# VectorE, not TensorE, sums the gathered relation messages in a graph network kernel

## The chip, the cores and the metric

The kernel runs on one core of one Trainium2 chip. The metric is the time on the device in microseconds, from one launch that computes everything. The engines are named as the profile names them: PE is TensorE, DVE is VectorE, ACT is ScalarE, POOL is GpSimd, SP is SyncE.

## What is computed

The reference runs three layers of a graph network over 3125 nodes with 128 features and 103125 edges, then adds the input and normalises. In each layer every node sums two things over its incoming edges:

```
ht = einsum('nd,rdo->nro', h, W_rel[l]);  msg = ht[src, etype]
h_rel = segment_sum(msg, dst) + h @ W_loop[l] + b_rel[l]
z = (h @ W_gat[l]).reshape(n, H, DH)
e = leaky_relu(el[src] + er[dst], 0.2);  ex = exp(e - segment_max(e, dst)[dst])
h_gat = segment_sum(ex / segment_sum(ex, dst)[dst] * z[src], dst) + b_gat[l]
hc = concatenate([h_rel, h_gat]) @ W_fuse + b_fuse
h = relu(hc * gate if l == 0 else hc)
```

The plain sum of `msg` is the "relation sum"; the sum weighted by the attention `ex` is the "attention sum". The change concerns the relation sum.

## The kernel before

**Tables and gathers.** For each layer a table in HBM has one row per node and relation: 128 numbers of the message, 128 of z and 4 attention terms `el` (`ROW` = 260 numbers). Nodes are ranked by degree and put in 25 tiles of 128, one node to a partition. A tile needs as many slots as its largest node has edges; a slot is one row per partition. POOL fetches one slot of a tile with one indirect DMA (`gather`, L640).

**Groups.** Slots are worked in groups of 8 in the buffers `A` and `B`, and at a tile's end a tail: `t8` (8 slots, in `scratch`) and `t7` (up to 7 slots, gathered in pieces of 4, 2 and 1, `pieces`). A tile is therefore A, B, perhaps one or more further pairs A, B, then perhaps t8 and t7. In all there are 348 groups. An empty slot of `t7` has its attention term set to `LEAST`, so that its weight is zero.

**One group.** The DVE (`group`, L1454 on) waits until the slots have landed, makes the logits in six short steps (`raw`, `top`, `leaky`, `peak`, the kept top, `logit`, L1471 to L1483), and waits for ACT to turn them into weights `wgt` (L863) and weight columns of `zx` (L864). Then it multiplies z by the weights into `zx` (L1487), rescales the running sum `acc` (L1489), does the `meanwhile` work of that group, and when PE has summed the group (`s_gat`) adds PE's sum to `acc` (L1495). PE (`group`, L1103 on) waits for the landed slots and adds their messages into `ps_rel`, one matmul with the identity per slot (`relation_sum`, L1112); then it waits for `zx` and sums it over the slots in the same way into `ps_gat` (L1126). A float32 matmul is two records in the trace, so a group of 8 has 16 of each kind. The first matmul of L1126 releases the buffer to POOL (`s_free`), the last one signals `s_gat`.

**Tile and table work.** At a tile's end DVE inverts the denominators and forms `hr` (relation sum plus loop term, L1509) and `hg` (L1513). The rest of that tile, its epilogue, is done inside the next tile: PE transposes `hr` and `hg` (L1135, L1136) behind the relation sum of A, ACT evacuates them, PE multiplies by W_fuse; in layer 0 a gate follows (L1151) behind the relation sum of B; in layers 0 and 1 PE then computes the next table's rows (`ps_z` L948, `ps_tab` L958) around the third and fourth group. ACT evacuates these in program order with the weights of the groups, so that a group's weights can stand behind them. `stage_tails`, called in A's `meanwhile`, copies the indices of the tail, fills `t7` (L1436) and signals `s_tail`; POOL waits for that before it gathers a tail.

**Order.** Nothing reorders this: each engine's instructions stand in the order in which its block writes them, with semaphores between. POOL's gathers go on as long as the next buffer is free.

## Time and profile before

| | |
|---|---|
| median of 3 runs | 4862.06 us (4856.94 to 4863.91) |
| the profiled execution | 4824.77 us, of which the span of instructions is 4823.2 us |
| busy, share of the span | PE 49%, PE weight loads 41%, DVE 25%, ACT 11%, POOL 53% |
| DMA | 517.47 MB, mean 107 GB/s |

The page gives each engine's busy time and its share of the span, the span in 40 slices, the chain of work that ended last, and the costliest groups of instructions. In the chain, "issue" is time in which the engine waited for nothing that the profile shows, and "another core or an unknown queue" (also "remote") is a wait whose releasing signal came at a time at which the profile knows no instruction that ended; this program has one core. The end of a matmul in the records is modelled; the time at which its signal arrives is not.

### The profile page before, as it was taken

Reading aid. Unit: us, or ns where it says so; the run is one execution under the profiler, and the core shown is the slowest. Engines: PE = TensorE matmul, PEld = TensorE weight load, DVE = VectorE, ACT = ScalarE, POOL = GpSimd, SP = SyncE. Lnnn points to the kernel's source line nnn. Section 1 sums busy time; section 2 is a strip of 40 time slices with the busy share of each in tenths; the row PEclk is TensorE's granted clock in tenths of the full one; section 3 lists DMA queues with packets and bytes.
Section 4 is the critical chain, followed back from the end, with each engine's and each line's share of the span. In section 5 each row is a group of like instructions: output and inputs, shape, how many; then the busy total and the mean of one; then the engine's idle time right before and its main releaser. Section 6 shows DMA issues by size and latency. Waiting matters only on the chain.

```text
span 4823.2 us, 47995 instructions
## 1 busy us (share of the span) xinstructions
PE 2344.4 (49%) x12390; PEld 1963.7 (41%) x12391; DVE 1207.1 (25%) x4912; ACT 538.0 (11%) x1448; POOL 2532.9 (53%) x2681
## 2 busy tenths in 40 slices
PE   6744545455555554444554554553444444433444
PEld 4334444344443434344444443443434444333443
DVE  5212222222222221222222212221222222222232
ACT  4410111111111110011111111110000000000000
POOL 0354555555555445555555655545556555554553
PEclk9876677777777776677777767776767666666666
DMA  6753333333333333333334333334223222222222
GB/s 221 286 158 85 106 108 117 110 121 114 118 112 110 119 106 82 110 94 112 116 115 127 120 110 109 125 98 109 73 75 85 79 74 70 72 76 68 73 71 54
DMA packets 152522, 517.47 MB, mean 107 GB/s; under 512 B 45704, under 2 KB 53464, under 8 KB 139680
## 3 DMA queue, kind: packets, MB, share of 16 engines
q0 software_dynamic: 132384, 452.73, 32.9%
q1 hardware_dynamic: 20096, 64.25, 3.6%
q8 instruction: 18, 0.29, 0.0%
q14 instruction: 24, 0.20, 0.0%
HBM read 351.66 MB, written 165.18 MB: 107 GB/s over the span
## 4 chain that ended last, share of the span: by engine, by line
another core or an unknown queue 36%; issue 23%; PE 18%; DVE 13%; ACT 4%; DVEq 4%; DMA 2%; POOL 1%; SPq 0%; ACTq 0%; POOLq 0%; PEldq 0%
PE ps_gat L1126 10%; DVE zx L1487 5%; PE ps_tab L958 3%; PE ps_rel L1112 2%; ACT rows L890 1%; ACT rows L789 1%; DVE top L1474 1%; DVE raw L1471 1%; ACT ps_cnt L863 1%; PE ps_cnt L1009 1%; DMA xin<-in_x 1%; DVEq L396 1%; POOL meta_nat L640 1%; DVE acc L1495 1%
## 5 line engine op out<-in xcount | busy, mean ns | idle before, releaser
L1126 PE MATMUL ps_gat<-zx,ident 128*128 128x132 f32 x5442 | 935.3, 340 | 1287.1 <-DVE zx L1487 945.2
L640 POOL DMA_INDIRECT meta_nat<-table,stage_head x1200 | 1139.6, 950 | 695.8 <-issue 385.4
L1126 PEld LDWEIGHTS ps_gat<-zx,ident 128*128 128x128 f32 x5442 | 859.1, 244 | 1368.7 <-DVE zx L1487 1005.2
L1112 PE MATMUL ps_rel<-meta_nat,ident 128*128 128x128 f32 x4428 | 763.3, 339 | 590.5 <-DVE hg L1513 231.2
L1112 PEld LDWEIGHTS ps_rel<-meta_nat,ident 128*128 128x128 f32 x4428 | 717.5, 250 | 659.2 <-issue 410.4
L1495 DVE TENSOR_TENSOR acc<-acc,ps_gat 128x132 f32<-128x132 f32 x348 | 101.8, 292 | 2291.8 <-remote 1734.6
L640 POOL DMA_INDIRECT meta_nat<-table,stage_mid_A x384 | 364.0, 948 | 550.4 <-PE ps_gat L1126 428.0
L958 PE MATMUL ps_tab<-wrel,hT 128*128 128x512 f32 x600 | 385.1, 767 | 211.5 <-issue 143.6
L640 POOL DMA_INDIRECT scratch<-table,stage_t x312 | 295.9, 948 | 362.0 <-issue 362.0
L1487 DVE TENSOR_TENSOR zx<-meta_nat,ps_cnt 128x1024 f32<-128x1024 f32 (+1 forms) x309 | 369.2, 1195 | 430.9 <-ACT ps_cnt L863 361.8
L640 POOL DMA_INDIRECT meta_nat<-table,stage_mid_B x384 | 364.2, 948 | 133.7 <-issue 114.3
L863 ACT ACTIVATE ps_cnt<-logit 128x36 f32<-128x36 f32 (+1 forms) x348 | 70.9, 204 | 2666.4 <-DVE logit L1483 1951.7
L958 PEld LDWEIGHTS ps_tab<-wrel,hT 128*128 128x128 f32 x600 | 134.7, 246 | 364.4 <-issue 246.1
L640 POOL DMA_INDIRECT meta_nat<-table,stage_t x246 | 233.3, 948 | 79.1 <-issue 79.1
L789 ACT ACTIVATE rows<-ps_tab 128x512 f32<-128x512 f32 x300 | 175.4, 599 | 567.0 <-remote 297.1
L948 PE MATMUL ps_z<-wz,hT 128*128 128x264 f32 (+1 forms) x150 | 58.0, 476 | 226.1 <-issue 117.3
L890 ACT ACTIVATE rows<-ps_z 128x2112 f32<-128x2112 f32 x50 | 96.6, 1931 | 638.4 <-remote 387.4
L706 POOL DMA_INDIRECT table<-rows,stage_id x50 | 48.9, 978 | 184.4 <-ACT meta L797 175.3
L1112 PEld LDWEIGHTS ps_rel<-scratch,ident 128*128 128x128 f32 x624 | 105.1, 258 | 74.5 <-issue 74.2
L1112 PE MATMUL ps_rel<-scratch,ident 128*128 128x128 f32 x624 | 106.6, 342 | 54.9 <-DMA scratch<-table,stage_t 51.8
L948 PEld LDWEIGHTS ps_z<-wz,hT 128*128 128x128 f32 x150 | 29.7, 237 | 249.5 <-issue 128.6
L1487 DVE TENSOR_TENSOR zx<-scratch,ps_cnt 128x1024 f32<-128x1024 f32 x39 | 47.7, 1222 | 242.3 <-ACT ps_cnt L863 205.8
(192 smaller groups left out, 1653.4 us busy)
## 6 DMA issues: line engine op xcount, KB each, us to landing
table<-rows SPq DMA_DIRECT2D x50, 1040.0 KB
meta_nat<-table,stage_head POOLq DMA_INDIRECT x1200
meta_nat<-table,stage_mid_A POOLq DMA_INDIRECT x384
meta_nat<-table,stage_mid_B POOLq DMA_INDIRECT x384
scratch<-table,stage_t POOLq DMA_INDIRECT x312
meta_nat<-table,stage_t POOLq DMA_INDIRECT x246
meta<-meta_ranked POOLq DMA_DIRECT2D x1, 3250.0 KB
xin<-in_x SPq DMA_DIRECT2D x48, 64.0 KB, 4.4
```

The source lines that it names most:

```text
L396: n = eng.value_load(tile_slots[0:1, bass.ds(t, 1)], min_val=PAIR, max_val=E)
L640: pool.indirect_dma_start(out=slots[b][:, k, :], out_offset=None, in_=table[l % 2], in_offset=bass.IndirectOffsetOnAxis(ap=indices[:, k:k ...
L706: pool.indirect_dma_start(out=table[(l + 1) % 2][0:NP_ * R, :].rearrange("(n r) f -> n (r f)", r=R), out_offset=bass.IndirectOffsetOnAxis( ...
L789: s.activation(rows[k][:, c * RC:(c + 1) * RC, 0:D], ps_tab[c % 2][:].rearrange("p (r f) -> p r f", r=RC), ACT.Copy).then_inc(s_bank[(c + ...
L863: s.activation(wgt[:, 8 - K:9, :, 0], logit[:, 8 - K:9, :], ACT.Exp).then_inc(s_wgt, 1)
L890: s.activation(rows[last][:, :, D:ROW], bc(ps_z[:, 0:D + H], R), ACT.Copy)
L948: pe.matmul(ps_z[:, 0:width], hT[k][:], wz[:, l, 0:width], start=True, stop=True).then_inc(s_z_ps, 1)
L958: pe.matmul(ps_tab[c % 2][:], hT[k][:], wrel[:, l, c * RC * D:(c + 1) * RC * D], start=True, stop=True).then_inc(s_chunk[c], 1)
L1112: pe.matmul(ps_rel[:, 0:D], ident[:], slots[b][:, k, 0:D], start=first and k == 0, stop=True, skip_group_check=True)
L1126: mm = pe.matmul(ps_gat[:, 0:W], ident[:], zs[:, 8 - K + k, :], start=(k == 0), stop=(k == K - 1))
L1487: v.tensor_tensor(zx[:, lo:8, :, 0:DH], slots[b][:, :, D:2 * D].rearrange("p k (h c) -> p k h c", h=H), wgt[:, lo:8].to_broadcast([P, K, H ...
L1495: v.tensor_tensor(acc[:], acc[:], ps_gat[:, 0:H * EX].rearrange("p (h e) -> p h e", h=H), ALU.add).then_inc(s_acc, 1)
```

## The change

PE no longer sums the messages. On DVE each group now has a `tensor_reduce` over the slots, placed between `logit` and `zx`; for a tile's first group it writes the new SBUF buffer `rel`, for every other group it writes a part into the PSUM bank that held `ps_rel`, and a second instruction adds this part to `rel` after the `meanwhile` work. `hr` reads `rel`. Since a reduce over `t7` reads all 7 slots, `stage_tails` also fills the message columns of `t7` with zeros, ahead of `s_tail`. PE has no wait for landed slots any more, nor the wait for `hr`'s reader ahead of a tile's first sum.

```diff
--- before.py
+++ after.py
@@ -227,6 +227,7 @@
         logit = sb("logit", [P, 9, H])
         zx = sb("zx", [P, 9, H, EX])
         acc = sb("acc", [P, H, EX])
+        rel = sb("rel", [P, D])
         rden = sb("rden", [P, H, 1])
         hg = sb("hg", [P, H, DH])
         hr = sb("hr", [P, D])
@@ -251,6 +252,7 @@
         ps_cnt = ps("ps_cnt", [P, 512])
         ps_xT = [ps_rel[:, 0:P]] * 2 + [ps_mix[:, 0:P]] * 2
         mix = [ps_mix[:, 128 * i:128 * i + 128] for i in range(4)]
+        rel_part = ps_rel[:, 0:D]
         wgt = ps_cnt[:, 0:9 * H].rearrange("p (k h o) -> p k h o", h=H, o=1)
 
 
@@ -333,6 +335,7 @@
         s_peak = sem("peak_ready")
         s_keep = sem("top_kept")
         s_logit = sem("logits_ready")
+        s_part = sem("relation_part_summed")
         s_wgt = sem("weights_ready")
         s_wcol = sem("weight_columns_ready")
         s_zx = sem("weighted_z_ready")
@@ -1100,22 +1103,8 @@
             for b in GROUPS:
                 pe.sem_inc(s_free[b], 1)
 
-            def group(b, first=False, mid=None, n_slots=None):
+            def group(b, mid=None):
                 K = GK[b]
-
-                def relation_sum(b):
-                    pe.wait_ge(s_landed[b], n_land[b])
-                    pe.reg_add(n_land[b], n_land[b], 16 * GK[b])
-                    if first:
-                        pe.wait_ge(s_h2, n_h)
-                    for k in range(GK[b]):
-                        pe.matmul(ps_rel[:, 0:D], ident[:], slots[b][:, k, 0:D], start=first and k == 0,
-                                  stop=True, skip_group_check=True)
-
-                if b == "t7":
-                    pieces(pe, n_slots, relation_sum)
-                else:
-                    relation_sum(b)
                 if mid:
                     mid()
                 pe.wait_ge(s_zx, n_g)
@@ -1168,7 +1157,7 @@
                 n, pairs, in_first = load_slots(pe, t)
                 split = previous and l < L - 1
                 if previous:
-                    group("A", first=True, mid=lambda: transpose_sums(l))
+                    group("A", mid=lambda: transpose_sums(l))
                     fuse(l)
                     group("B", mid=lambda: gate(l))
                     half_table(l)
@@ -1180,11 +1169,11 @@
                         with pe.If(in_first > 1):
                             group("B")
                 else:
-                    group("A", first=True)
+                    group("A")
                     group("B")
                 pair_loops(pe, 2 if split else 1, pairs, in_first, n_lowered, n_land,
                            lambda hub: (group("A"), group("B")))
-                tail_groups(pe, n, lambda b: group(b, n_slots=n))
+                tail_groups(pe, n, group)
                 pe.reg_add(n_h, n_h, 1)
 
             for l in range(L):
@@ -1433,8 +1422,8 @@
                     dve.reg_alu(piece_at, piece_at, dve.snap(in_first * PAIR + t * ELL), ALU.add)
                     copy_indices(stage_tail[b][:], piece_at, K)
 
-                ins = v.memset(slots["t7"][:, :, 2 * D:ROW], LEAST)
-                ins.then_inc(s_tail, 1)
+                v.memset(slots["t7"][:, :, 0:D], 0.0)
+                v.memset(slots["t7"][:, :, 2 * D:ROW], LEAST).then_inc(s_tail, 1)
 
             def stage_next_head(t):
                 dve.wait_ge(s_head, n_head)
@@ -1451,7 +1440,7 @@
                     dve.reg_add(n_id_out, n_id_out, 16)
                 v.tensor_copy(stage_id[last][:].bitcast(I32), id_u[:, bass.ds(t, 1)].bitcast(I32)).then_inc(s_id, 1)
 
-            def group(b, stage=False, n_slots=None, meanwhile=None):
+            def group(b, stage=False, n_slots=None, meanwhile=None, first=False):
 
                 K = GK[b]
                 lo = 8 - K
@@ -1482,6 +1471,8 @@
                 dve.wait_ge(s_peak, n_g)
                 v.tensor_tensor(logit[:, lo:9], leaky[:, lo:9], peak[:].to_broadcast([P, K + 1, H]), ALU.subtract
                                 ).then_inc(s_logit, 1)
+                v.tensor_reduce(rel[:] if first else rel_part, slots[b][:, :, 0:D].rearrange("p k d -> p d k"), AX.X,
+                                ALU.add).then_inc(s_part, 1)
                 dve.wait_ge(s_keep, n_g)
                 dve.wait_ge(s_wgt, n_g)
                 v.tensor_tensor(zx[:, lo:8, :, 0:DH], slots[b][:, :, D:2 * D].rearrange("p k (h c) -> p k h c", h=H),
@@ -1490,6 +1481,9 @@
                                 ).then_inc(s_scaled, 1)
                 if meanwhile:
                     meanwhile()
+                if not first:
+                    dve.wait_ge(s_part, n_g)
+                    v.tensor_tensor(rel[:], rel[:], rel_part, ALU.add)
                 dve.wait_ge(s_scaled, n_g)
                 dve.wait_ge(s_gat, n_g)
                 v.tensor_tensor(acc[:], acc[:], ps_gat[:, 0:H * EX].rearrange("p (h e) -> p h e", h=H), ALU.add
@@ -1506,7 +1500,7 @@
 
                 dve.wait_ge(s_acc, n_g)
                 v.reciprocal(rden[:], acc[:, :, DH:EX]).then_inc(s_rden, 1)
-                v.tensor_tensor(hr[:], ps_rel[:, 0:D], meta[:, bass.ds(t, 1), M_LOOP:M_X].rearrange("p o f -> p (o f)"),
+                v.tensor_tensor(hr[:], rel[:], meta[:, bass.ds(t, 1), M_LOOP:M_X].rearrange("p o f -> p (o f)"),
                                 ALU.add)
                 dve.wait_ge(s_rden, n_rd)
                 dve.reg_add(n_rd, n_rd, 1)
@@ -1564,7 +1558,7 @@
                 n, pairs, in_first = load_slots(dve, t)
                 start_tile(t)
                 dve.reg_mov(mid_at, t * ELL + PAIR)
-                group("A", stage=True, meanwhile=lambda: stage_tails(t, n, in_first))
+                group("A", stage=True, meanwhile=lambda: stage_tails(t, n, in_first), first=True)
                 group("B", stage=True, meanwhile=lambda: between(l, t, previous))
                 if previous is not None:
                     epilogue(l, previous)
```

The order on PE at the start of a tile in the loop over tiles of layer 0 (`ps_rel` is the relation sum, `ps_gat` the attention sum, `ps_mix` the epilogue of the tile before). Before:

```order
L1108 REGISTER_ALU [waits slots_A_landed]
L1112 MATMUL ps_rel<-meta_nat,ident 128x128 [waits node_sums_ready]
L1112 MATMUL ps_rel<-meta_nat,ident 128x128 x7
L1135 MATMUL ps_mix<-ident,hr 128x128 [waits node_sums_ready]
L1136 MATMUL ps_mix<-ident,hg 128x128
L1126 MATMUL ps_gat<-zx,ident 128x132 [waits weight_columns_ready,weighted_z_ready]
L1126 MATMUL ps_gat<-zx,ident 128x132 x7
L1131 REGISTER_ALU
L1141 MATMUL ps_mix<-hrT,wfuse 128x128 [waits transposed_sums_ready]
L1142 MATMUL ps_mix<-hgT,wfuse 128x128
L1108 REGISTER_ALU [waits slots_B_landed]
L1112 MATMUL ps_rel<-meta_nat,ident 128x128 x8
```

And now:

```order
L1124 MATMUL ps_mix<-ident,hr 128x128 [waits node_sums_ready]
L1125 MATMUL ps_mix<-ident,hg 128x128
L1115 MATMUL ps_gat<-zx,ident 128x132 [waits weight_columns_ready,weighted_z_ready]
L1115 MATMUL ps_gat<-zx,ident 128x132 x7
L1120 REGISTER_ALU
L1130 MATMUL ps_mix<-hrT,wfuse 128x128 [waits transposed_sums_ready]
L1131 MATMUL ps_mix<-hgT,wfuse 128x128
L1140 MATMUL ps_mix<-hc,wgate 128x128 [waits fused_ready]
```

The relation sums and their waits for landed slots are gone, and the transposes and the gate stand directly behind what they need.

The order on DVE in a group that is not a tile's first, here A of a further pair. Before:

```order
L1481 COPY raw<-top 128x4 [waits leaky_ready]
L1483 TENSOR_TENSOR logit<-leaky,peak 128x36 [waits peak_ready]
L1487 TENSOR_TENSOR zx<-meta_nat,ps_cnt 128x32x32 [waits weights_ready,top_kept]
L1489 TENSOR_TENSOR acc<-acc,ps_cnt 128x132
L1495 TENSOR_TENSOR acc<-acc,ps_gat 128x132 [waits group_sum_ready,sums_rescaled]
```

And now:

```order
L1470 COPY raw<-top 128x4 [waits leaky_ready]
L1472 TENSOR_TENSOR logit<-leaky,peak 128x36 [waits peak_ready]
L1474 TENSOR_REDUCE ps_rel<-meta_nat 128x128
L1478 TENSOR_TENSOR zx<-meta_nat,ps_cnt 128x32x32 [waits weights_ready,top_kept]
L1480 TENSOR_TENSOR acc<-acc,ps_cnt 128x132
L1486 TENSOR_TENSOR rel<-rel,ps_rel 128x128 [waits relation_part_summed]
L1489 TENSOR_TENSOR acc<-acc,ps_gat 128x132 [waits group_sum_ready,sums_rescaled]
```

The reduce stands ahead of the instruction that PE waits for; the addition stands behind it, ahead of the one that waits for PE.

The order on DVE at the end of `stage_tails`, in a tile's first group. Before:

```order
L1433 ISA
L1418 COPY stage_t<-ell 128x1
L1436 MEMSET meta_nat 128x7x4
L1495 TENSOR_TENSOR acc<-acc,ps_gat 128x132 [waits group_sum_ready,sums_rescaled]
L1497 REGISTER_ALU
```

And now:

```order
L1422 ISA
L1407 COPY stage_t<-ell 128x1
L1425 MEMSET meta_nat 128x7x128
L1426 MEMSET meta_nat 128x7x4
L1489 TENSOR_TENSOR acc<-acc,ps_gat 128x132 [waits group_sum_ready,sums_rescaled]
L1491 REGISTER_ALU
```

The new fill of 7 x 128 numbers stands ahead of the one that signals `s_tail`.

## Rows read from the trace of the kernel before

**Rows 1.** The page: span, and busy time of each engine.

```profile
span 4823.2 us, 47995 instructions
...
PE 2344.4 (49%) x12390; PEld 1963.7 (41%) x12391; DVE 1207.1 (25%) x4912; ACT 538.0 (11%) x1448; POOL 2532.9 (53%) x2681
```

**Rows 2.** The page: the chain that ended last, by engine and by line.

```profile
another core or an unknown queue 36%; issue 23%; PE 18%; DVE 13%; ACT 4%; DVEq 4%; DMA 2%; POOL 1%; SPq 0%; ACTq 0%; POOLq 0%; PEldq 0%
PE ps_gat L1126 10%; DVE zx L1487 5%; PE ps_tab L958 3%; PE ps_rel L1112 2%; ACT rows L890 1%; ACT rows L789 1%; DVE top L1474 1%; DVE raw L1471 1%; ACT ps_cnt L863 1%; PE ps_cnt L1009 1%; DMA xin<-in_x 1%; DVEq L396 1%; POOL meta_nat L640 1%; DVE acc L1495 1%
```

**Rows 3.** Busy time by stretch: first to last `hg` of layers 0, 1 and 2.

```profile
core 0: us, PE busy (x) PEld busy (x) DVE busy (x) ACT busy (x) POOL busy (x), PEclk, DMA share, GB/s
397.00:1761.00 1364.00, 710.59 (x3688) 582.74 (x3688) 323.14 (x1385) 175.47 (x456) 752.40 (x792) 0.73 0.37 112
1901.00:3258.00 1357.00, 676.71 (x3640) 567.74 (x3640) 311.88 (x1337) 167.20 (x432) 752.18 (x792) 0.72 0.37 112
3395.00:4804.00 1409.00, 614.60 (x3450) 568.02 (x3450) 388.87 (x1721) 55.31 (x264) 753.12 (x792) 0.68 0.28 74
```

**Rows 4.** Groups by line: busy us, mean ns, idle us before, and its releasers.

```profile
L1126 PE MATMUL ps_gat<-zx,ident 128*128 128x132 f32 x5442 | 935.3, 340 | 1287.1 <-DVE zx L1487 945.2 <-issue 341.7
...
L1112 PE MATMUL ps_rel<-meta_nat,ident 128*128 128x128 f32 x4428 | 763.3, 339 | 590.5 <-DVE hg L1513 231.2 <-DMA meta_nat<-table,stage_mid_A 154.8 <-DMA meta_nat<-table,stage_head 97.6
...
L640 POOL DMA_INDIRECT meta_nat<-table,stage_mid_B x384 | 364.2, 948 | 133.7 <-issue 114.3 <-PE ps_gat L1126 12.6 <-remote 5.9
...
L1112 PE MATMUL ps_rel<-scratch,ident 128*128 128x128 f32 x624 | 106.6, 342 | 54.9 <-DMA scratch<-table,stage_t 51.8 <-issue 3.2
...
L1495 DVE TENSOR_TENSOR acc<-acc,ps_gat 128x132 f32<-128x132 f32 x348 | 101.8, 292 | 2291.8 <-remote 1734.6 <-PE ps_gat L1126 514.8 <-issue 42.5
```

**Rows 5.** Timeline at the start of a tile of layer 1: start us, us, engine, line.

```profile
2545.54 3.79 PE L1112 MATMUL ps_rel<-meta_nat,ident 128*128 128x128 f32 x16 [1.11 <-DVE hg L1513]
...
2548.70 1.22 DVE L1487 TENSOR_TENSOR zx<-meta_nat,ps_cnt 128x1024 f32<-128x1024 f32 x1 [0.34 <-ACT ps_cnt L863]
...
2549.12 0.42 PE L1135 MATMUL ps_mix<-ident,hr 128*128 128x128 f32 x1
...
2549.98 2.07 PE L1126 MATMUL ps_gat<-zx,ident 128*128 128x132 f32 x16 [0.23 <-DVE zx L1487]
...
2551.24 0.94 POOL L640 DMA_INDIRECT meta_nat<-table,stage_mid_A  x1 [4.40 <-PE ps_gat L1126]
...
2552.15 0.29 DVE L1495 TENSOR_TENSOR acc<-acc,ps_gat 128x132 f32<-128x132 f32 x1 [1.71 <-PE ps_gat L1126]
```

**Rows 6.** Groups by line and form, DVE: reduces and a fill of known sizes.

```profile
L1316 DVE TENSOR_REDUCE rank<-scratch 128x4 f32<-128x512 f32 x6 | 4.1, 678 | 0.0
...
L1390 DVE MEMSET meta_nat<- 128x1820 f32 x1 | 1.6, 1575 | 0.3 <-issue 0.3
...
L1316 DVE TENSOR_REDUCE rank<-scratch 128x1 f32<-128x128 f32 x1 | 0.3, 286 | 0.0
```

**Rows 7.** Timeline, layer 2: first and last of a run of 22 gathers, and PE.

```profile
4426.64 0.94 POOL L640 DMA_INDIRECT scratch<-table,stage_t  x1 [9.18 <-issue]
...
4430.04 2.07 PE L1126 MATMUL ps_gat<-zx,ident 128*128 128x132 f32 x16 [0.26 <-DVE zx L1487]
...
4438.28 3.76 PE L1112 MATMUL ps_rel<-scratch,ident 128*128 128x128 f32 x16 [6.18 <-DMA scratch<-table,stage_t]
...
4452.95 0.95 POOL L640 DMA_INDIRECT meta_nat<-table,stage_head  x1 [0.30 <-issue]
4456.31 0.29 DVE L1495 TENSOR_TENSOR acc<-acc,ps_gat 128x132 f32<-128x132 f32 x1 [24.22 <-remote]
```

**Rows 8.** The line that fills `t7`, and who waited for it (us, times).

```profile
L1436 DVE MEMSET meta_nat<- x75: 82/82/82, 293.7 to 4782.4; 128x28 f32 x75
...
  POOL scratch L640: 275.1, 27
```

**Rows 9.** Timeline, layer 2: the sum of the t8 group behind an idle PE.

```profile
4462.86 3.89 PE L1126 MATMUL ps_gat<-zx,ident 128*128 128x132 f32 x16 [20.82 <-DVE zx L1487]
```

## The prediction

> **What bounds the kernel now.** I read the page first, for how full the engines are. POOL is busy 53% of the span, PE 49%, DVE 25% [rows 1]: none is full, so the time is set by a chain of waits. In the chain that ended last [rows 2], 36% of the span is waits whose end the profile ties to no instruction. The `ps_gat` sums hold 10%, `zx` 5%, and the relation sums, which the change takes off PE, 2%.
>
> Next, the costliest groups. The DVE instruction that adds PE's sum to `acc` (L1495) is behind 2291.8 us of idle time, 1734.6 of them "remote" [rows 4]. The timeline shows what these are. In layer 2 a run of 22 gathers goes from 4426.64 to 4453.90, one each 1.25 us. The sum of group B is recorded at 4430.04 and takes 2.07 us, yet DVE gets its signal only at 4456.31, 24.22 us after it began to wait and 2.4 us after the last gather was issued [rows 7]. At the start of such a run the signal is punctual: a run begins at 2551.24, a sum ends at 2552.05 and DVE goes on at 2552.15 [rows 5]. So I take it that PE's signals are held while POOL's gathers run on, and are let go when the run ends. A tile then alternates between a run of gathers and, behind it, a serial stretch of group after group (DVE, ACT, DVE, PE) until a buffer comes free. In layer 1 such a stretch ends with the sum of A, and POOL, idle for 4.40 us, goes on [rows 5].
>
> The table of stretches says whether PE's work matters. Layer 2 has no table products: PE is busy 614.60 us there against 710.59 and 676.71, and yet it takes 1409 us against 1364 and 1357 [rows 3]. Less work for PE did not shorten a layer.
>
> **The change, part by part.**
>
> (a) *The reduce.* Two reduces on DVE, of 128 and 512 numbers, take 0.286 and 0.678 us [rows 6], so 1.02 ns a number more; 1024 numbers come to 1.20 us. They are read with a stride, but `zx` reads 1024 of the same rows with the same stride in 1.22 us [rows 5]. The reduce stands where DVE waited 0.34 us for ACT's weights [rows 5]. So it delays `zx` by 0.86 us, less a little because DVE instructions overlap at their ends: I take 0.8. That counts where `zx` is on the chain: 5% of 4823.2 us is 241 us, or some 200 of the 348 groups at 1.2 us each. 200 x 0.8 = **+160 us**. At the rate of the fill below (0.87 ns a number, 0.89 us less 0.34) it would be 200 x 0.55 = 110, and with every group on the chain 348 x 0.8 = 278. In the other 148 groups DVE waits for PE's held signal or for weights that stand behind ACT's evacuation of the table, and the reduce is free. Should that cover go, these are the groups that make 278 of 160.
>
> (b) *The fill of `t7`.* 1820 numbers took 1.575 us [rows 6], so 7 x 128 = 896 numbers take 0.78 us. DVE waits 1.71 us for PE in that place [rows 5], so DVE itself loses nothing. But POOL waits for the signal behind the fill before it gathers a tail: 27 times, 275.1 us in all [rows 8]. 27 x 0.78 = **+21 us**; nothing, if a buffer is what it then waits for.
>
> (c) *The addition to `rel`.* A DVE instruction of this size takes 0.29 us (L1495) [rows 4]. It stands where DVE waits at least 1.71 us for PE [rows 5]. With the fill and the stage copies still inside that wait: 0. Without that cover it would be 273 x 0.29, or 79 us.
>
> (d) *The relation sums leave PE.* They are 763.3 + 106.6 us of its busy time [rows 4], but 2% of the chain, 96 us. In the rows of layer 1 they run from 2545.54 to 2549.33, ahead of the transposes at 2549.12, while `zx` ends at 2549.92 and the sum of A starts at 2549.98: nothing on the path waited for them [rows 5]. Where they are on the chain, something stands close behind: the weights, the evacuation, the landed slots. Between 0 and -96 I take half, **-48 us**.
>
> (e) *PE's clock.* The granted clock is 0.73, 0.72 and 0.68 of 2.4 GHz in the three layers [rows 3], a mix of 1.2 and 2.4. The sum of A ran at 2.4 GHz, in 2.07 us, right behind 3.79 us of relation sums [rows 5]; the sum of the t8 group, behind 20.82 us of idle time, ran at 1.2 GHz in 3.89 [rows 9]. Without the relation sums A's sum loses what ran ahead of it. It costs 1.82 us where it happens: 75 tiles x 1.82 = 137 us at most. POOL's release comes from the first matmul of the sum, though, and B's signal is held anyway. I take **+30 us**.
>
> (f) *The waits of PE for landed slots* go; DVE waits for the same slots, so nothing new waits for them. The gate of layer 0 no longer stands behind B's landing on PE, but ACT's tanh for it still stands behind B's weights. 0.
>
> The sum is 160 + 21 + 0 - 48 + 30 = +163 us. The profiled execution took 4824.77 us, so 4988 by its own time; the median of the runs is 37 us above it, 4862.06, which gives **5025 us**.
>
> **The rivals.**
>
> *One, PE's queue was the brake: much faster.* The held signals could be PE's own work in line. Then they would shrink by the share taken away, 869.9 of 2344.4 us of busy time, 37% of 1734.6 us, or 642; with (a) and (b), 4862 - 642 + 181 = 4400 us. For it speaks that PE is nearly the fullest engine. Against it: in the 24.22 us of rows 7 PE had one sum of 2.07 us left and 3.76 us of relation sums behind it, and layer 2 is no faster for its smaller load [rows 3]. Two pages of the Trainium skill lead to this rival. "Perfetto Trace Analysis", Identifying the Most-Contended Engine, says to take work first from the engine with the highest occupancy, for TensorE by its weight loads; here those are 41%, less than POOL, which the change leaves alone. "SBUF — State Buffer", Who interferes with whom, says that DMA never contends with a compute engine; by that rule gathers could not hold PE, and the wait would be PE's own. The trace speaks against it with the 24.22 us beside 5.83 us of work.
>
> *Two, the reduce is covered: a little faster.* If most `zx` on the chain are held by ACT or by a late signal ahead of them, (a) is 0 and (d) is whole: 4862 + 21 - 96 = 4787 us. It decides from about 90 groups on the path downwards, where 90 x 0.8 + 21 is what (d) can give. For it speaks that only the inferred chain gives the 200; against it, that in rows 5 and in the stretch behind rows 7 the path runs through `zx` with an idle time of 0.34 us.
>
> *Three, B's release falls into the held stretch: slower still.* A's sum at 1.2 GHz (1.82 us) and the reduce (0.8) move B's first matmul later into POOL's run. If its signal is then held, POOL stops after A's 8 gathers, waits 2.4 us past the last, and about 0.8 more to start. There are 384/8 = 48 further pairs [rows 4]: 48 x 3.3 = 158 us on top, 5183 us.
>
> *Four, the parts cancel:* 4862 us. That the change doesn't do what it says can be set aside: the order shows the matmuls gone and the reduces there.
>
> **How the numbers follow.** The forecast gets 0.53, rival one 0.10, two 0.17, three 0.12, four 0.08. A difference of 0.2%, 10 us, is about what a measurement of this kernel can tell from none. Slower: 0.53 + 0.12 = 0.65; same 0.08; faster 0.27. The range reaches down to rival two and up to rival three, 4787 to 5183 us. It takes in (a) at 110 and at 278, (e) at 0 and at 137, and leaves out rival one and what lies past the ends of two and three.
>
> **What would show each step.** The reduce: about 1.2 us each, 348 times, and DVE's idle time before `zx` at 0 in most groups instead of 0.34. The fill: 0.78 us, 75 times. The addition: 273 times, with DVE still waiting for PE behind it. PE's busy time down by about 870 us or less, its granted clock lower, more sums of 3.9 us. POOL's waits for a freed buffer longer by about the sum, while the "remote" time before L1495 stays near 1730 us. The prediction is wrong in its ground if that time falls by hundreds: then the relation sums did hold PE. It is wrong in its size if POOL's waits don't grow.

## The result and the profile after

| | before | after |
|---|---|---|
| median | 4859.50 us (4807.91 to 4863.91, 4 runs) | 4945.76 us (4931.97 to 4946.98, 4 runs) |
| span of the profiled execution | 4823.2 us | 4943.0 us |
| busy: PE, PE weight loads, DVE, POOL | 49%, 41%, 25%, 53% | 38%, 30%, 39%, 51% |

The change makes the kernel slower: the ratio is 1.0243, with an interval of 1.0196 to 1.0291. The forecast was 5025 us and its range 4787 to 5183. The two medians of the table give a smaller ratio, 1.0178, below that interval; how the two come together is not on record. The kernel before scatters: its medians in the comparisons below are 4811.42 to 4825.11 us, and against those the change would be at 1.025 to 1.028. So the size lies somewhere between 1.8% and 2.8%; the direction is not in doubt.

The page after: span and busy time, and the chain by engine and by line. They answer to [rows 1] and [rows 2].

```profile
span 4943.0 us, 37627 instructions
...
PE 1897.3 (38%) x7338; PEld 1497.0 (30%) x7339; DVE 1926.1 (39%) x5608; ACT 529.5 (11%) x1448; POOL 2524.9 (51%) x2681
...
another core or an unknown queue 27%; issue 26%; PE 20%; DVE 16%; DVEq 5%; ACT 3%; POOL 1%; DMA 1%; SPq 0%; ACTq 0%; POOLq 0%; PEldq 0%
```

PE gave back 447 us of busy time, not 870, because what is left runs at a lower clock: the attention sum alone takes 340 us more. DVE took on 719 us. The span grew by 120 us: most of the added DVE time was hidden. In the chain the waits that no instruction explains fell from 36% to 27%; "issue", PE and DVE rose.

The groups of instructions on DVE and PE after, by line and form: busy us, mean ns, idle us before, releasers. They answer to [rows 4].

```profile
L1474 DVE TENSOR_REDUCE ps_rel<-meta_nat 128x128 f32<-128x1024 f32 x171 | 330.9, 1935 | 0.0
L1474 DVE TENSOR_REDUCE rel<-meta_nat 128x128 f32<-128x1024 f32 x75 | 144.6, 1928 | 0.0
L1474 DVE TENSOR_REDUCE ps_rel<-meta_nat 128x128 f32<-128x896 f32 x63 | 111.4, 1768 | 0.0
L1489 DVE TENSOR_TENSOR acc<-acc,ps_gat 128x132 f32<-128x132 f32 x348 | 101.7, 292 | 1840.7 <-remote 1050.6 <-PE ps_gat L1115 737.7 <-issue 52.4
L1486 DVE TENSOR_TENSOR rel<-rel,ps_rel 128x128 f32<-128x128 f32 x273 | 76.8, 281 | 3.0
L1425 DVE MEMSET meta_nat<- 128x896 f32 x75 | 60.4, 805 | 10.2
```

```profile
L1115 PE MATMUL ps_gat<-zx,ident 128*128 128x132 f32 x5442 | 1275.4, 425 | 2521.6 <-DVE zx L1478 1804.4 <-issue 717.2
```

Three things differ from what was foreseen. A reduce of 1024 numbers takes 1.93 us, not 1.20. The waits of unknown release before the addition to `acc` shrank by 684 us instead of staying near 1730. And a matmul of the attention sum takes 425 ns on average where it took 340.

The table of stretches after, again first to last `hg` of each layer (against [rows 3]).

```profile
397.00:1787.00 1390.00, 585.29 (x2120) 448.62 (x2120) 548.04 (x1603) 171.21 (x456) 750.08 (x792) 0.63 0.37 109
1931.00:3330.00 1399.00, 550.83 (x2072) 436.01 (x2072) 536.27 (x1555) 165.31 (x432) 750.02 (x792) 0.64 0.36 109
3468.00:4922.00 1454.00, 460.44 (x1880) 411.58 (x1880) 610.92 (x1935) 52.66 (x264) 751.15 (x792) 0.55 0.27 71
```

The layers grew by 26, 42 and 45 us, 113 of the 120. PE is busy 125, 126 and 154 us less in them, at a granted clock of 0.63, 0.64 and 0.55 instead of 0.73, 0.72 and 0.68.

The timeline after, right behind the ninth `hg` of layer 1. The lines of [rows 5] stand behind the eleventh; those of the same tile before follow below.

```profile
2481.05 0.20 DVE L1472 TENSOR_TENSOR logit<-leaky,peak 128x36 f32<-128x36 f32 x1
2481.16 1.92 DVE L1474 TENSOR_REDUCE rel<-meta_nat 128x128 f32<-128x1024 f32 x1
...
2483.00 1.21 DVE L1478 TENSOR_TENSOR zx<-meta_nat,ps_cnt 128x1024 f32<-128x1024 f32 x1
...
2484.26 3.89 PE L1115 MATMUL ps_gat<-zx,ident 128*128 128x132 f32 x16 [5.15 <-DVE zx L1478]
...
2485.84 0.94 POOL L643 DMA_INDIRECT meta_nat<-table,stage_mid_A  x1 [11.31 <-PE ps_gat L1115]
...
2488.26 0.29 DVE L1489 TENSOR_TENSOR acc<-acc,ps_gat 128x132 f32<-128x132 f32 x1 [2.59 <-PE ps_gat L1115]
```

The same tile before:

```profile
2434.19 0.20 DVE L1483 TENSOR_TENSOR logit<-leaky,peak 128x36 f32<-128x36 f32 x1
...
2434.72 1.22 DVE L1487 TENSOR_TENSOR zx<-meta_nat,ps_cnt 128x1024 f32<-128x1024 f32 x1 [0.34 <-ACT ps_cnt L863]
...
2436.00 2.55 PE L1126 MATMUL ps_gat<-zx,ident 128*128 128x132 f32 x16 [0.24 <-DVE zx L1487]
...
2437.58 0.95 POOL L640 DMA_INDIRECT meta_nat<-table,stage_mid_A  x1 [10.16 <-PE ps_gat L1126]
...
2438.66 0.29 DVE L1495 TENSOR_TENSOR acc<-acc,ps_gat 128x132 f32<-128x132 f32 x1 [2.20 <-PE ps_gat L1126]
```

The two show what the change does in one group. After, `logit` ends at 2481.25 and `zx` starts 1.75 us later; before, it was 0.33 us. PE, which has stood still for 5.15 us, sums A in 3.89 us (at 1.2 GHz), where it took 2.55. POOL, waiting for A's buffer, goes on 4.59 us after the end of `logit` instead of 3.19, and DVE gets to its addition after 7.01 us instead of 4.27. POOL's whole wait, 11.31 us against 10.16, begins with the end of its last run and says less.

### The profile page after: what moved, and what is told of

It reads as the page before. It is cut to its first block, busy times and chain, and to the rows that moved or that the text cites. A ratio compares the mean times of both kernels' runs of the same rounds, so it can differ in the third digit from the quotient of the medians.

```text
span 4943.0 us, 37627 instructions
## 1 busy us (share of the span) xinstructions
PE 1897.3 (38%) x7338; PEld 1497.0 (30%) x7339; DVE 1926.1 (39%) x5608; ACT 529.5 (11%) x1448; POOL 2524.9 (51%) x2681
## 4 chain that ended last, share of the span: by engine, by line
another core or an unknown queue 27%; issue 26%; PE 20%; DVE 16%; DVEq 5%; ACT 3%; POOL 1%; DMA 1%; SPq 0%; ACTq 0%; POOLq 0%; PEldq 0%
PE ps_gat L1115 16%; DVE zx L1478 6%; PE ps_tab L961 2%; DVE ps_rel L1474 2%; ACT rows L893 1%; DVE top L1463 1%; DVEq L399 1%; DVE raw L1460 1%; PE ps_cnt L1012 1%; ACT rows L792 1%; DVE acc L1489 1%; PE ps_z L951 1%; DVE raw L1470 1%; DVE logit L1472 1%
## 5 line engine op out<-in xcount | busy, mean ns | idle before, releaser
L1115 PE MATMUL ps_gat<-zx,ident 128*128 128x132 f32 x5442 | 1275.4, 425 | 2521.6 <-DVE zx L1478 1804.4
L1115 PEld LDWEIGHTS ps_gat<-zx,ident 128*128 128x128 f32 x5442 | 1179.3, 324 | 2680.0 <-DVE zx L1478 1918.9
L1489 DVE TENSOR_TENSOR acc<-acc,ps_gat 128x132 f32<-128x132 f32 x348 | 101.7, 292 | 1840.7 <-remote 1050.6
L1474 DVE TENSOR_REDUCE ps_rel<-meta_nat 128x128 f32<-128x896 f32 (+1 forms) x234 | 442.2, 1890 | 0.0
L643 POOL DMA_INDIRECT meta_nat<-table,stage_t x246 | 232.6, 946 | 101.5 <-issue 101.5
L1474 DVE TENSOR_REDUCE rel<-meta_nat 128x128 f32<-128x1024 f32 x75 | 144.6, 1928 | 0.0
L1124 PE MATMUL ps_mix<-ident,hr 128*128 128x128 f32 x75 | 32.1, 427 | 235.9 <-DVE hg L1507 194.6
L1460 DVE TENSOR_TENSOR raw<-meta_nat,er_cur 128x32 f32<-128x32 f32 (+1 forms) x309 | 61.0, 197 | 108.5 <-issue 103.9
L1480 DVE TENSOR_TENSOR acc<-acc,ps_cnt 128x132 f32<-128x132 f32 x348 | 99.3, 285 | 0.0
L1124 PEld LDWEIGHTS ps_mix<-ident,hr 128*128 128x128 f32 x75 | 12.7, 169 | 256.7 <-DVE hg L1507 214.1
```

The lines of the kernel that those rows point to most:

```text
L643: pool.indirect_dma_start(out=slots[b][:, k, :], out_offset=None, in_=table[l % 2], in_offset=bass.IndirectOffsetOnAxis(ap=indices[:, k:k ...
L1115: mm = pe.matmul(ps_gat[:, 0:W], ident[:], zs[:, 8 - K + k, :], start=(k == 0), stop=(k == K - 1))
L1460: v.tensor_tensor(raw[:, lo:8], slots[b][:, :, 2 * D:ROW], er_cur[:].to_broadcast([P, K, H]), ALU.add).then_inc(s_raw, 1)
L1474: v.tensor_reduce(rel[:] if first else rel_part, slots[b][:, :, 0:D].rearrange("p k d -> p d k"), AX.X, ALU.add).then_inc(s_part, 1)
L1480: v.tensor_tensor(acc[:], acc[:], wgt[:, 8].to_broadcast([P, H, EX]), ALU.mult).then_inc(s_scaled, 1)
L1489: v.tensor_tensor(acc[:], acc[:], ps_gat[:, 0:H * EX].rearrange("p (h e) -> p h e", h=H), ALU.add).then_inc(s_acc, 1)
```

## The experiments

Ratios are to the kernel before, run on the same chip in the same comparison, whose own median of before stands beside a time. In the expectations, "Theory A" is: the relation sums stood in PE's way and the reduce costs its full price, some 320 us. "Theory B" is: taking them off PE is worth at most 50 us, and most of the reduce is covered.

### The two halves of the change apart

*Without the reduces* (the change, with the reduces and the additions to `rel` taken out; the relation sum is left out of the result; the fill of `t7` stays).

```diff
-                v.tensor_reduce(rel[:] if first else rel_part, slots[b][:, :, 0:D].rearrange("p k d -> p d k"), AX.X,
-                                ALU.add).then_inc(s_part, 1)
...
-                if not first:
-                    dve.wait_ge(s_part, n_g)
-                    v.tensor_tensor(rel[:], rel[:], rel_part, ALU.add)
```

> The change without its reduces and additions on VectorE; TensorE's relation sums stay away too, so the relation sum is left out of the result altogether (the fill of t7 stays). It prices what taking the sums off TensorE gives by itself. Theory A (the relation sums did stand in the way: the 'remote' time before the addition to acc fell from 1734.6 to 1050.6 us with the change, and the reduce, at 1.93 us instead of 1.20, costs about 200 x 1.6 = 320 us): about 4860 - 220 = 4640 us, 4580 to 4720. Theory B (TensorE's relief gives no more than 50 us; the remote time only moved behind a slower VectorE, and the reduce costs about 120 us because it is mostly covered): 4810 to 4880 us.

Measured: 4793.27 us against 4825.11, ratio 0.9964 (0.9923 to 1.0005). Taking the relation sums off PE is worth 17 us, between 37 us and nothing. The granted clock fell to 0.621.

*DVE's part alone* (the kernel before, PE's sums kept, plus the reduce, addition and fill of the change, whose result nothing reads).

```diff
+                v.tensor_reduce(rel[:] if first else rel_part, slots[b][:, :, 0:D].rearrange("p k d -> p d k"), AX.X,
+                                ALU.add).then_inc(s_part, 1)
...
+                    v.tensor_tensor(rel[:], rel[:], rel_part, ALU.add)
```

> The kernel before, with the change's reduces, additions and fill on VectorE as dead work, and with TensorE's relation sums kept as the ones that count. It prices VectorE's part by itself and, against the change, TensorE's relief with VectorE's load in place. Theory A: 4860 + 320 = about 5180 us, 5100 to 5250. Theory B: about 4980 us, 4940 to 5010, within 50 us of the change.

Measured: 4967.27 us, ratio 1.0342 (1.0230 to 1.0454). DVE's part costs about 165 us (111 to 219). Its part sums go to SBUF here, since PE's sum keeps the PSUM bank. So the loss is DVE's. With DVE's load in place PE's relief gives back about a percent (1.0342 against 1.0243), but the two intervals overlap.

### The place of the reduce

The reduce stands behind `zx` and so beside PE's attention sum; DVE then releases the buffer, which PE's first matmul had released, and does the addition to `rel` ahead of the `meanwhile` work.

```diff
                                 wgt[:, lo:8].to_broadcast([P, K, H, DH]), ALU.mult).then_inc(s_zx, 1)
+                v.tensor_reduce(rel[:] if first else rel_part, slots[b][:, :, 0:D].rearrange("p k d -> p d k"), AX.X,
+                                ALU.add).then_inc(s_part, 1)
...
+                dve.wait_ge(s_part, n_g)
+                dve.sem_inc(s_free["t7" if b == "t7" else b], 1)
```

> The change with the reduce moved behind the instruction that makes zx, so that it runs while TensorE sums; the buffer is then released to GpSimd by VectorE, behind the reduce, and no longer by TensorE's first matmul. If it is the path logit, zx, TensorE's sum that the reduce lengthens (both theories name it), about 1.6 us come back in each group on the chain, but the release to GpSimd comes about as late as in the change (zx end + 2.2 us against reduce + zx end + 0.6). Theory A: 4720 to 4850 us. Theory B: 4850 to 4920 us. If the release to GpSimd alone sets the time: as the change, 4930 to 4960 us.

Measured: 4871.36 us, ratio 1.0139 (1.0043 to 1.0234): about 1% better than the change, the two intervals overlapping at their ends.

```profile
L643 POOL DMA_INDIRECT meta_nat<-table,stage_mid_A x384 | 364.2, 949 | 578.3 <-DVEq L1481 479.7 <-issue 98.0 <-DVE stage_mid_B L1405 0.6
L1488 DVE TENSOR_TENSOR acc<-acc,ps_gat 128x132 f32<-128x132 f32 x348 | 99.8, 287 | 1736.0 <-remote 1475.2 <-PE ps_gat L1115 181.9 <-issue 76.2
```

These two groups of the kernel with the late reduce show both sides. DVE hardly waits for PE's sum where the signal is punctual (181.9 us instead of 737.7): the reduce fills that time. But the unexplained waits are longer than in the change, 1475.2 us against 1050.6, so that its idle time in that place falls by only 105 us in all. POOL now waits for DVE's release (L1481), which stands behind the reduce.

### Are the late signals PE's own backlog?

The kernel before, with two of the eight matmuls of each attention sum; the others are left out of that sum.

```diff
-                for k in range(K):
+                for k in (0, K - 1):
                     mm = pe.matmul(ps_gat[:, 0:W], ident[:], zs[:, 8 - K + k, :], start=(k == 0),
```

> The kernel before with only the first and the last of a group's matmuls of the attention sum; 6 of 8 (5 of 7 in t7) are left out of that sum. It asks whether TensorE's late signals are frozen signals or slow work. If they are only held while gathers run (the prediction's view), the recorded durations go, up to 6/8 of the 10% of the chain, 360 us, and the remote time stays above 1400 us: 4450 to 4650 us. If TensorE works slowly while gathers run, so that the late signal is a backlog of matmuls, the remote time falls to a third as well: below 4300 us.

Measured: 4483.49 us, ratio 0.9322 (0.9233 to 0.9412).

```profile
L1495 DVE TENSOR_TENSOR acc<-acc,ps_gat 128x132 f32<-128x132 f32 x348 | 101.8, 293 | 1920.2 <-remote 1674.3 <-PE ps_gat L1126 193.7 <-issue 49.4
```

With a quarter of the matmuls the unexplained waits are still 1674.3 us (1734.6 before): they are no backlog of slow attention sums. Nor are they one of relation sums, without which they were 1461.1 us. What went is the punctual part, 514.8 to 193.7 us. A length of PE work that lies between `zx` and `acc` counts; the relation sums, beside the path, don't.

### How much of a reduce counts

*Two reduces* (the change, with a second one whose result nothing reads):

```diff
+                v.tensor_reduce(rel2[:], slots[b][:, :, 0:D].rearrange("p k d -> p d k"), AX.X, ALU.add)
```

> The change with a second reduce of the same rows behind the first, its result unused. A reduce is 1.93 us; the first one, with the addition and the fill, cost about 165 us. Theory B (a longer VectorE step takes part of its own price out of the waits that are held while gathers run, whatever its size): the second costs about what the first did, 0.25 us for each of its 1.93: about 5110 us, remote time before the instruction that adds to acc down by another 300. Rival A (the first one used up the cover, and what comes now counts in full on some 200 groups): 200 x 1.93 = 386, about 5330 us, and the remote time stays near 1050.

Measured: 5287.68 us against 4811.42, ratio 1.0987 (1.0953 to 1.1021). By the ratios the second one cost 0.0744 x 4820 = 359 us of the 672 that 348 reduces take: the rival's time was nearly right, theory B's wrong. Of the signs it was theory B's that came: the unexplained waits fell by another 268 us, to 782.1, where the rival had them stay near 1050.

*Half a reduce:*

```diff
-                v.tensor_reduce(rel[:] if first else rel_part, slots[b][:, :, 0:D].rearrange("p k d -> p d k"), AX.X,
+                v.tensor_reduce(rel[:] if first else rel_part, slots[b][:, 0:4, 0:D].rearrange("p k d -> p d k"), AX.X,
```

> The change with a reduce over the first four slots alone (512 numbers, about 1.0 us instead of 1.93); the messages of the other slots are left out of the relation sum. Measured so far: no reduce 4793, one 4946, two 5288 us; so the second cost 341 us, all of its 1.93 us on 177 groups, and the first with the addition only 153. Theory C (a cover of about 1.07 us on those groups, then full price): half a reduce lies inside the cover, 4795 to 4815 us, ratio below 1.000. Rival (the first one is cheap because a part of every microsecond is taken out of held signals, 0.41 of it counting): 4793 + 0.97 x 153/1.93 = 4870 us, ratio 1.012.

Measured: 4838.15 us against 4817.82, ratio 1.0055 (1.0030 to 1.0080). Neither: the first half is not free, and not a straight share of the whole. The four kernels together, by their ratios since they come from different comparisons (1.93 us is the mean of a full reduce, 1.02 of a half one), with the waits of unknown release before the addition to `acc`:

| reduce per group | ratio | added, of 4820 us | per added us of reduce | unexplained waits |
|---|---|---|---|---|
| none | 0.9964 | | | 1461.1 us, 129 times |
| 1.02 us | 1.0055 | 44 us | 43 us | 1263.3, 121 |
| 1.93 us | 1.0243 | 91 us | 100 us | 1050.6, 110 |
| 2 x 1.93 us | 1.0987 | 359 us | 186 us | 782.1, 90 |

The last column in the view of waits (us, times, longest), for half a reduce, the change and two reduces:

```profile
DVE acc L1489 <- remote: 1263.3, 121, 30.1
```

```profile
DVE acc L1489 <- remote: 1050.6, 110, 31.4
```

```profile
DVE acc L1491 <- remote: 782.1, 90, 25.0
```

(The step from none also holds the addition, 0.28 us, which lies in a wait; the intervals make each step uncertain by some 25 us.) One microsecond more counts in 43 groups at first, then in 100, and at last in 186 of 348. The number of groups on the path is no constant of the kernel; it grows with what is added, while the unexplained waits become fewer and shorter. The upper steps hang on the change's own ratio: with 1.0178 in its place they would be 65 and 202 instead of 100 and 186; the order stays. That these waits are the cover is the reading that fits; no run isolates them.

### The fill of t7

```diff
-                v.memset(slots["t7"][:, :, 0:D], 0.0)
```

> The change without the fill of the message columns of t7; empty slots of t7 put stale messages into the relation sum. The prediction's step (b): 27 tails wait for it, 21 us less, about 4925 us, 0.4%. Rival: a buffer or VectorE's later start is what those tails wait for, 0, 4946 us. POOL's wait for the tail signal (397.4 us, 27 times, 275.1 before the change) says how much of its growth is the fill's: 22 us by the first, and the other 100 come from the reduce ahead of it in the same group.

Measured: 4935.35 us, ratio 1.0256 (1.0226 to 1.0287), the change's own being 1.0243. Empty slots leave stale messages in the sum here. The fill costs nothing that can be seen, but the intervals are some 20 us wide each way, so 21 us can't be told from nothing by this run. POOL's waits for the line that signals the tail were 397.4 us after the change,

```profile
  POOL scratch L643: 397.4, 27
```

275.1 before [rows 8], 372.6 without the fill and 382.0 without the reduces. The 24.8 us that the fill adds to them are what was foreseen for the wait (22). And the wait grew by 107 us already when only PE's sums had gone and the fill had come, yet that kernel was no slower. POOL's wait moved from one place to another.

### PE's clock

The kernel without reduces, with matmuls of constants on PE in the place of the relation sums (the relation sum is left out of the result).

```diff
+                for k in range(K):
+                    pe.matmul(ps_rel[:, 0:D], ident[:], ident[:], start=True, stop=True)
```

> The kernel without reduces and additions (the relation sum left out of the result), with matmuls of the identity in the place of the relation sums on TensorE: as many, as large, but waiting for nothing. Without them it took 4793 us at a granted clock of 0.62; with the true sums (the kernel before) 4825 at about 0.71. If the waits for landed slots made the difference, it stays at 4793 or falls to 4760 by the warmer clock (fewer sums of 3.9 us; 1.8 us each on up to 75 tiles). If the matmuls themselves are what stood in the way, it is 4825 or above, with a clock of 0.7 and a mean of 340 ns for the matmuls of the attention sum.

Measured: 4821.39 us against 4811.42, ratio 1.0038 (0.9999 to 1.0076), clock 0.723. The attention sum's matmuls fell from 420 to 358 ns, 245 us of PE's time, and yet the kernel is 0.0074 slower than without them, 36 us, with an uncertainty of some 27. So the matmuls themselves, not their waits for landed slots, are what the relation sums cost, and it is more than the warmer clock gives back. The two are not taken apart by it.

### A shorter attention sum

If PE's work between `zx` and `acc` counts, a part of *that* sum belongs on DVE. The kernel before, with its relation sums on PE; DVE adds the upper four slots of `zx` to the lower four:

```diff
                                 wgt[:, lo:8].to_broadcast([P, K, H, DH]), ALU.mult).then_inc(s_zx, 1)
+                dve.wait_ge(s_zx, n_g)
+                v.tensor_tensor(zx[:, lo:4], zx[:, lo:4], zx[:, lo + 4:8], ALU.add).then_inc(s_pairs, 1)
...
-                for k in range(K):
+                for k in range(4):
```

> The kernel before (relation sums on TensorE), with VectorE adding the upper four slots of zx to the lower four (528 numbers, about 0.6 us) and TensorE summing four instead of eight. Two eighths of the matmuls alone gave -342 us (6.8%), so four eighths should give about -228; VectorE's 0.65 us more cost 0.25 to 0.58 us for each of 348 groups, 57 to 200 us. Theory B (the low end): about 4655 us, 0.965. Rival (all of it counts, since it stands behind zx where TensorE waits): about 4800, 0.995. Remote time stays above 1400 in both.

Measured: 4592.18 us against 4811.42, ratio 0.9556 (0.9519 to 0.9592), better than either theory had it. Then the same once more, halves and quarters, and two matmuls on PE:

```diff
+                dve.wait_ge(s_pairs, n_g)
+                v.tensor_tensor(zx[:, lo:lo + 2], zx[:, lo:lo + 2], zx[:, lo + 2:lo + 4], ALU.add).then_inc(s_quads, 1)
```

> The kernel before with VectorE adding halves (measured 0.69 us) and then quarters of zx (264 numbers, about 0.4 us), TensorE summing two slots' columns instead of eight. With halves 4592 us. Two matmuls less are 0.5 us at full clock and 0.97 at half, against 0.4 us and a wait between two VectorE instructions. If TensorE's matmuls are taken mostly at full clock on the path: even, 4590 us (0.955). If at half clock: 0.5 us less on 177 groups, 4500 us (0.937). Worse than 4620 if the new wait costs more than 0.3 us.

Measured: 4548.94 us against 4817.82, ratio **0.9439** (0.9401 to 0.9478), between the two cases foreseen, and the best on these chips of the kernels that compute everything.

```profile
L1501 DVE TENSOR_TENSOR acc<-acc,ps_gat 128x132 f32<-128x132 f32 x348 | 101.7, 292 | 1619.6 <-remote 1381.7 <-PE ps_gat L1127 127.9 <-issue 104.1
L1492 DVE TENSOR_TENSOR zx<-zx 128x528 f32<-128x528 f32 (+1 forms) x348 | 238.3, 685 | 37.3 <-issue 1.6
L1494 DVE TENSOR_TENSOR zx<-zx 128x264 f32<-128x264 f32 x348 | 150.9, 434 | 12.0
```

1.12 us of DVE per group replace six matmuls, and DVE's punctual waits for PE fall from 514.8 us [rows 4] to 127.9.

*Both sums*: the change, with the late reduce and the halves.

```diff
+                v.tensor_tensor(zx[:, lo:4], zx[:, lo:4], zx[:, lo + 4:8], ALU.add).then_inc(s_pairs, 1)
+                v.tensor_reduce(rel[:] if first else rel_part, slots[b][:, :, 0:D].rearrange("p k d -> p d k"), AX.X,
+                                ALU.add).then_inc(s_part, 1)
```

> Both ideas together: relation sums on VectorE behind zx and the halves, so that VectorE reduces while TensorE sums; TensorE sums four instead of eight. Adding the parts: halves gave -219 us, the change with the late reduce +60: 4650 us, 0.97. A theory by which TensorE's relation sums stand in the way would give below 4592 (0.955). A theory by which a shorter attention sum leaves the late reduce of 1.93 us uncovered (it hid beside 2.07 to 3.9 us of matmuls, now 1.0 to 1.9) gives 4650 + 177 x 0.9 = 4810, 1.00.

Measured: 4633.62 us, ratio 0.9618 (0.9548 to 0.9688). The parts add up, nearly (0.97). The relation sums are still better left on PE, with an uncertainty as large as the difference from 0.9556. DVE's unexplained waits before the addition are 663.5 us in this kernel, by far the fewest on these chips. So they do shrink when PE has neither the relation sums nor half of the attention sum and DVE comes later as well; which of these it is, no run shows.

### No PE in a group at all

The change, with the attention sum wholly on DVE (halves, quarters, eighths), and the buffer released by DVE.

```diff
-                for k in range(K):
-                    mm = pe.matmul(ps_gat[:, 0:W], ident[:], zs[:, 8 - K + k, :], start=(k == 0),
...
+                v.tensor_tensor(zx[:, lo:4], zx[:, lo:4], zx[:, lo + 4:8], ALU.add).then_inc(s_pairs, 1)
+                dve.sem_inc(s_free[b], 1)
...
+                v.tensor_tensor(acc[:], acc[:], zx[:, lo], ALU.add
```

> The change carried to its end: VectorE also does the attention sum (halves, quarters, eighths of zx: 0.69, about 0.4 and 0.29 us, then the addition to acc from SBUF), and releases the buffer itself. TensorE has no part in a group any more and keeps transposes, W_fuse, gate and tables. Theory H (the signals that TensorE sends while gathers run come late, and VectorE then finds landed groups undone behind the run): VectorE's idle time before the instruction that adds to acc, 1840.7 us in the change, falls below 100; VectorE needs some 8 us a group against about 10 us of gathers, so POOL waits less: its idle time before gathers, 2005 us, halves, 3900 to 4200 us, ratio 0.81 to 0.87. Rival (the held time only stands beside gathers that run anyway, and what counts is the matmul time on the path, so that this is one more step after the quarters): the last two matmuls and the handshake go, 0.8 us on 177 groups, but the reduce stays ahead of zx, 130 to 150 us: about 4550 us, 0.94.

Measured: 3737.24 us (3735.86 to 3738.49) against 3638.79 (3637.33 to 3640.28), ratio 1.0271 (1.0257 to 1.0285). The kernel before took 3638.79 us on this chip where it took 4811 to 4862 in every other comparison. The groups of this kernel:

```profile
L645 POOL DMA_INDIRECT meta_nat<-table,stage_mid_A x384 | 379.8, 989 | 124.5 <-issue 94.4 <-DVEq L1478 19.2 <-DVE stage_mid_B L1399 11.0
L1489 DVE TENSOR_TENSOR acc<-acc,zx 128x132 f32<-128x132 f32 x348 | 103.0, 296 | 36.2
```

As theory H has it, DVE waits 36.2 us before the addition, and POOL's idle time before its gathers is 802 us (384.0 + 124.5 + 117.0 + 101.5 + 74.9). But the kernel before, with PE's signals in it, is faster still there, so the run doesn't show that these are what PE's late signals cost: neither theory's ratio came out. There is no profile of the kernel before on that chip.

The trace of this kernel has one more thing to say. PE still sends ACT the signals for the table's `rows`, and gathers run meanwhile as before. In the kernel before, 684.5 us of ACT's waits for them end without an instruction that explains it; here none do, and in the whole trace no wait does.

```profile
L789 ACT ACTIVATE rows<-ps_tab 128x512 f32<-128x512 f32 x300 | 175.4, 599 | 567.0 <-remote 297.1 <-PE ps_tab L958 161.2 <-issue 107.6
L890 ACT ACTIVATE rows<-ps_z 128x2112 f32<-128x2112 f32 x50 | 96.6, 1931 | 638.4 <-remote 387.4 <-issue 162.0 <-PE ps_z L948 89.0
```

```profile
L794 ACT ACTIVATE rows<-ps_tab 128x512 f32<-128x512 f32 x300 | 172.7, 596 | 122.8 <-PE ps_tab L963 122.1 <-DMA table<-rows 0.3
L895 ACT ACTIVATE rows<-ps_z 128x2112 f32<-128x2112 f32 x50 | 96.1, 1922 | 152.8 <-PE ps_z L953 152.8
```

In the traces from the other chips these waits of ACT are never below 370 us, whatever PE had to do. So on this chip, with this kernel, PE's signals come on time while gathers run. That speaks for the chip, and not the kernel, as what makes them late, and so for late signals as what costs the 1180 us between the chips. But this kernel also gives PE less to do, and a trace of the kernel before on this chip is missing: that step is argued, not shown. Also open are why the chips differ, and whether the change, or the quarters, keep their ratios there. The granted clock of the kernel before is 0.80 there and 0.72 elsewhere.

## Why the prediction was right, and where it was not

The direction was right, and the size came out at +2.4% (+1.8% by the medians) for +3.3%. The mechanism was right in that DVE's reduce stands on the path and costs more than PE's relief gives back. That the size is near owes much to luck, in (a). Step by step:

- **(a) The reduce: two errors that cancel.** The duration was taken as 1.20 us "since `zx` reads 1024 of the same rows with the same stride in 1.22". That step failed. The reduce takes 1.93 us, 0.73 more than foreseen. `zx` reads with the features innermost, 128 neighbouring numbers per slot; the reduce reads with the slots innermost, so each number lies 1040 bytes from the one before. That this is the reason is argued: the reduces of [rows 6] also make 1 or 4 long sums where this one makes 128 short ones, and no run changes the one without the other. The second error is the 200 groups on the path, taken from the chain as a constant. With 1.93 us the same working would have given 200 x (1.93 - 0.34) = 318 us; the change over the kernel without reduces is 1.0243 against 0.9964, 136 us, near the 160 of the sum by luck. At the margin the 200 was good: 186 groups paid in full for the second reduce. For the first microseconds it was far too high, 43 and 100.
- **(b) The fill.** 0.805 us, 75 times, as foreseen (0.78). It adds 24.8 us to POOL's waits for the tail's signal, about as foreseen; whether these reach the kernel's time, as 21 us or not at all, the run without it can't tell.
- **(c) The addition.** 273 times at 281 ns, with 3.0 us of idle time before them all; it lies in DVE's wait for PE, though no run took it away by itself.
- **(d) and (e) PE's relief and its clock.** Together -18 us by the prediction, or +3 with the fill; measured, with the fill, -17 (-37 to +2). The clock fell as foreseen (to 0.62), and the mean of the attention sum's matmuls rose from 340 to 425 ns. The -48 and the +30 are not shown apart, and their net only within those 20 us.
- **(f)** held: the kernel with constant matmuls waits for no landed slots, and is not faster than before.

**The signs.** The reduce, its count and the fall of DVE's idle time before `zx` were right in kind: the waits for ACT's weights fell in number from 237 to 45, though in time only from 567.6 to 451.9 us, since the long ones stayed. POOL's waits for PE's release grew by 84 us:

```profile
POOL meta_nat L643 <- PE ps_gat L1115: 709.6, 96, 20.8
```

It was 626.1, 72 times, before. But its waits of unknown release there fell from 149.6 to 8.5 us in the meantime, so that the wait for buffers did not grow as the prediction had it. POOL's idle time before its gathers grew by 184 us in all (1821.0 to 2004.6), 122 of them before those of t8, which wait for the tail's signal. The sign that should have held the ground did not: the unexplained time before the addition to `acc` fell from 1734.6 to 1050.6 us. The prediction read such a fall as "the relation sums did hold PE". The runs show another cause. DVE's part alone, with PE's sums in place, brings it to 1373.3; PE's relief alone to 1461.1; yet the first is slower and the second no faster. A signal that is late anyway is waited for less long when DVE comes to it later; this fits, and no run isolates it. This time is not a price, and its change alone says nothing of the kernel's.

**The held signals.** The prediction took it that PE's signals are let go when the run of gathers ends. That is so in [rows 7], but not in general. In the kernel before, over its whole timeline, 66 of the 160 unexplained waits (666 of 1734.6 us) end while the gathers go on at their step of 1.25 us. Here PE's sum is recorded at 3481.55, DVE gets the signal at 3498.27, and POOL doesn't stop:

```profile
3481.55 2.07 PE L1126 MATMUL ps_gat<-zx,ident 128*128 128x132 f32 x16 [0.25 <-issue]
...
3497.71 0.94 POOL L640 DMA_INDIRECT scratch<-table,stage_t  x1 [0.30 <-issue]
3498.27 0.29 DVE L1495 TENSOR_TENSOR acc<-acc,ps_gat 128x132 f32<-128x132 f32 x1 [14.68 <-remote]
...
3498.96 0.95 POOL L640 DMA_INDIRECT scratch<-table,stage_t  x1 [0.30 <-issue]
```

So the signals are late during gathers on these chips, but what lets them go is open.

**The rivals.** *One* (PE's queue was the brake) is refuted: PE's relief gave 0.4%, where 642 us were to come back. The rule of the Trainium skill, "Perfetto Trace Analysis", Identifying the Most-Contended Engine, is to work first on the engine with the highest occupancy, PE being judged by its weight loads; that puts POOL (53%) first and PE's weight loads (41%) next. The trace has the weight loads at 30% afterwards, with no gain. But PE's work between `zx` and `acc` was worth 5.6%. The engine was the right one; the work on it was not. *Two* (the reduce covered, slightly faster) is refuted: the reduce cost 136 us, what 86 groups at its full excess would (136/1.59), and PE's relief gave 17 us, not 96. *Three* (B's release held) did not come: POOL's waits for PE before `stage_mid_B` went from 12.6 [rows 4] to 13.9 us. *Four* is outside the interval.

## What to carry to other kernels

Ask of work that is to be moved whether it lies between two links of the chain or beside it: relation sums of 870 us beside it were worth 17 us, and three quarters of the attention sum, between two links, 5.6% net of what DVE then did. A count of groups "on the chain" is a price at the margin, and here the early microseconds cost less; to know how many, run the added step at half and at double length. And read which axis is innermost before a duration is borrowed from another instruction on the same data.

## What was not expected of the hardware

- A DVE reduce whose innermost step is 1040 bytes takes 1.02 us for 512 numbers, 1.77 for 896 and 1.93 for 1024: 1.8 ns a number more, where the contiguous ones of [rows 6] have 1.02. The half reduce reads as many numbers as the one of 678 ns in [rows 6], with another stride and in 128 sums instead of 4:

```profile
L1474 DVE TENSOR_REDUCE ps_rel<-meta_nat 128x128 f32<-128x512 f32 x234 | 239.5, 1024 | 0.0
```

  The Trainium skill, "SBUF — State Buffer", Door 1: The DMA port swizzle, says that accesses which cross to a new 16-byte line pay a penalty, and that four float32 numbers share one. The rows agree in direction: here every number is on a line of its own. How much of the difference is the stride's, no run shows.
- PE's signals came more than 20 us late while gathers ran [rows 7], and went on doing so with six of eight matmuls of the attention sum taken away (1674.3 us in all). On another chip the trace of the kernel without group sums on PE, with the same gathers, has no wait of unknown release at all, ACT's waits for PE included.
- One and the same program, the kernel before, had a median of 3638.79 us on one chip (9 runs within 3 us) and of 4811 to 4862 in the other comparisons. The ratios of this document but the last belong to the latter.
